# A graph network on one NeuronCore: TensorE's scatter loop in rounds of twenty groups, a different share of the marks for ScalarE, and three changed orders

## The reference, cut to what matters

```python
h = relu(layernorm(x)); x = x + gcn(h)         # L0: weighted sums over edges, degree normalised
h = relu(layernorm(x)); x = x + sage(h)        # L1: mean over edges, two 512x512 products, gate
h = relu(layernorm(x)); x = x + attention4(h)  # L2: four blocks of sparse attention and MLP
h = relu(layernorm(x)); x = x + gat(h)         # L3: two attention directions, fuse, batch norm
```

## Time and profile before

| What | us |
|---|---|
| Median of three runs (lowest and highest) | 882.91 (881.90 and 883.12) |
| The profiled execution's own time | 880.6 |
| Its span, from the first to the last instruction | 878.6 |
| PE busy, of the span | 826.9 (94%) |
| DVE busy | 623.1 (71%) |
| ACT busy | 460.1 (52%) |
| POOL busy | 493.6 (56%) |

### The profile page before, as it was taken

How to read it: one execution, slowest core, us unless ns; L and a number is a source line. 1 busy time by engine, 2 the same in 40 slices (tenths; PEclk the granted TensorE clock), 3 DMA queues, 4 the chain that set the end, 5 groups by cost and what they waited for, 6 DMA issues and landing times.

```text
span 878.6 us, 18172 instructions
## 1 busy us (share of the span) xinstructions
PE 826.9 (94%) x6778; PEld 723.7 (82%) x6778; DVE 623.1 (71%) x1271; ACT 460.1 (52%) x773; POOL 493.6 (56%) x542
## 2 busy tenths in 40 slices
PE   3999989999999999999999999999999999989896
PEld 2999868789898879998887989887898988875565
DVE  7998878964766683576766367577447667689996
ACT  5988675345762434565133466333447634256673
POOL 7354573678433577542466843266674338548871
PEclk9999999999999999999999999999999999999999
DMA  5000102233000142200024310003230002100121
GB/s 162 2 0 0 37 26 85 55 96 115 13 1 13 42 154 85 60 13 1 25 66 130 109 48 1 13 25 117 78 110 13 1 1 85 37 1 32 46 61 59
DMA packets 49760, 44.34 MB, mean 50 GB/s; under 512 B 6013, under 2 KB 37439, under 8 KB 49698
## 3 DMA queue, kind: packets, MB, share of 16 engines
q1 hardware_dynamic: 47234, 39.72, 15.2%
q10 hardware_dynamic: 2464, 3.80, 1.5%
HBM read 42.04 MB, written 1.33 MB: 49 GB/s over the span
## 4 chain that ended last, share of the span: by engine, by line
PE 70%; DVE 17%; ACT 6%; issue 3%; DMA 2%; DVEq 1%; POOL 0%; SPq 0%; ACTq 0%
PE psum L1822 20%; PE psum L1816 18%; PE psum L1927 13%; PE psum L1897 6%; PE psum L1846 5%; DVE arena L2349 3%; ACT arena L1618 2%; DVE arena L1013 2%; PE psum L2112 2%; PE psum L2109 2%; PE psum L1870 2%; PE psum L877 1%; PE psum L935 1%; DVE stats L2472 1%; DVE hot_dst L1050 1%
## 5 line engine op out<-in xcount | busy, mean ns | idle before, releaser
L1360 POOL TENSOR_SCALAR acc<-acc,rden,flag 128x628 f32<-128x628 f32 x80 | 69.5, 868 | 119.4 <-DVE rden L2345 119.4
L1927 PE MATMUL psum<-ringw,arena 128*128 128x512 f32 (+1 forms) x480 | 119.3, 397 | 4.0 <-DVE arena L2357 2.5
L1822 PE MATMUL psum<-arena 128*128 128x384 f32 (+5 forms) x675 | 115.8, 324 | 0.0
L1816 PE MATMUL psum<-arena,ringw 128*128 128x314 f32 x768 | 114.3, 310 | 0.1
L1816 PEld LDWEIGHTS psum<-arena,ringw 128*128 128x128 f32 x768 | 112.9, 190 | 1.5 <-DVE arena L2322 1.1
L1822 PEld LDWEIGHTS psum<-arena 128*128 128x128 f32 (+1 forms) x675 | 104.8, 189 | 7.1 <-DVE arena L2349 1.1
L1927 PEld LDWEIGHTS psum<-ringw,arena 128*128 128x128 f32 (+1 forms) x480 | 86.8, 186 | 25.6 <-DVE arena L2357 3.5
L1816 PE MATMUL psum<-arena 128*128 128x314 f32 (+1 forms) x480 | 87.7, 321 | 7.3 <-DVE arena L2349 6.9
L1816 PEld LDWEIGHTS psum<-arena 128*128 128x128 f32 (+1 forms) x480 | 70.5, 187 | 15.8 <-DVE arena L2349 14.1
L2322 DVE SCALAR_TENSOR_TENSOR arena<-psum,cols,arena 128x628 fp32r<-128x628 f32 x32 | 27.9, 872 | 75.8 <-ACT arena L1600 75.8
L1431 POOL TENSOR_TENSOR ringw<-raw,ringw 128x512 fp32r<-128x512 f32 x56 | 71.6, 1288 | 15.5 <-ACT ringw L1659 15.5
(11 more groups left out here) (313 smaller groups left out, 1840.6 us busy)
## 6 DMA issues: line engine op xcount, KB each, us to landing
raw<-in_L_gnn_m_w SPq DMA_DIRECT2D x16, 256.0 KB
xn<-in_L_gnn_m_w SPq DMA_DIRECT2D x16, 256.0 KB
raw<-in_L_gnn_wv SPq DMA_DIRECT2D x8, 256.0 KB
xn<-in_L_gnn_wv SPq DMA_DIRECT2D x8, 256.0 KB
raw<-in_L_gnn_wq SPq DMA_DIRECT2D x8, 256.0 KB
xn<-in_L_gnn_wq SPq DMA_DIRECT2D x8, 256.0 KB
raw<-in_L_gnn_wk SPq DMA_DIRECT2D x8, 256.0 KB
xn<-in_L_gnn_wk SPq DMA_DIRECT2D x8, 256.0 KB
```

The costliest lines, as they stand in the source:

```text
L1360: g.tensor_scalar(pbuf[:, k % 4, 0:NW], pbuf[:, k % 4, 0:NW], rden[:, k:k + 1], flag[:, 1, k % NT:k % NT + 1], ALU.mult, ALU.mult).then_in ...
L1816: ins = pe.matmul(big[buf(u)][0:l.shape[1], h, 0:HW], l, r[:, h * HW:(h + 1) * HW], start=(i == 0), stop=(i == len(terms) - 1))
L1822: ins = pe.matmul(to, l, r, start=(i == 0), stop=(i == len(terms) - 1))
L1927: ins = pe.matmul(brow(ROWBLK[f"{name}{t}"])[0:KEYS[t], :], l, r, start=(pieces[0] + i == 0), stop=(pieces[-1] == KT - 1 and i == len(term ...
```

## The change

There are five edits.

1. PE's scatter loop has bodies of ROUND = 20 groups instead of 4, so two rounds instead of ten.
2. ACT's and DVE's loops have bodies of SHARE = 8 groups. In the last group of each eight ACT makes chunks 2 and 3 and DVE only 0 and 1. ACT gets a third buffer for the extra Abs.
3. DVE's shift of `base_f` moves from the scatter's end to its start.
4. POOL makes `rstd_of` for tile 1 ahead of `left_rest(3)` instead of behind it, and `rstd_of` for tile 2 ahead of `bias_added(4)`.
5. In L3 PE waits for `h_read` and runs three idle products between `first_branch(0)` and `maxima(3)`.

```diff
--- before.py
+++ after.py
@@ -38,6 +38,13 @@
 assert all((i * PASS_MUL) >> 16 == i // WIN for i in range(NP + 1))
 HOT = 4
 assert NG % HOT == 0 and NT * 2 * WIN <= 512
+
+SHARE = 8
+assert NG % SHARE == 0 and SHARE % HOT == 0
+own_chunks = lambda g: CH - 1 - (g % SHARE == SHARE - 1)
+
+ROUND = 20
+assert NG % ROUND == 0 and ROUND % HOT == 0
 ACCW = NP + ROOM
 
 
@@ -274,7 +281,7 @@
         w_acc = adjacc[:, :, 1, 0:NP]
         hot_src = [m[:, :, :].rearrange("p t n -> p (t n)").bitcast(BF16)[:, b * CH * NP:(b + 1) * CH * NP].rearrange(
             "p (j n) -> p j n", j=CH) for m in (mask, z) for b in range(2)]
-        hot_abs = [mask[:, NT - 1, :].bitcast(BF16)[:, b * NP:(b + 1) * NP] for b in range(2)]
+        hot_abs = [mask[:, NT - 1, :].bitcast(BF16)[:, b * NP:(b + 1) * NP] for b in range(2)] + [xn[:, 1, D - NP // 2:D].bitcast(BF16)]
         hsum = hot_dst[:, :, :, :].rearrange("p b j n -> p (b j n)").bitcast(F32)[:, 0:NP].rearrange("p (t n) -> p t n", t=NT)
         cond_high = arena3[:, 0:NP]
         silu = xn[0:C16, :, :].rearrange("p b n -> p (b n)")[:, 0:NP]
@@ -912,6 +919,8 @@
             pe.wait_ge(am_read, 2)
             second_branch(1)
             first_branch(0)
+            pe.wait_ge(h_read, 2 * NT - 1)
+            idle_products(pe, 2 * NBIG, 3)
             maxima(EARLY)
             first_branch(1)
             pe.wait_ge(one_up, 2)
@@ -1515,11 +1524,12 @@
             for t in range(1, 4):
                 bias_added(t)
             left_rest(2)
-            rstd_of(LN_L1, NT)
+            for t in range(2):
+                rstd_of(LN_L1 + t, NT + t)
             left_rest(3)
-            rstd_of(LN_L1 + 1, NT + 1)
+            rstd_of(LN_L1 + 2, NT + 2)
             bias_added(4)
-            for t in range(2, NT):
+            for t in range(3, NT):
                 rstd_of(LN_L1 + t, NT + t)
             for k in range(KT):
                 right_rest(k)
@@ -1701,13 +1711,16 @@
             act.wait_ge(w_ready, 2)
             passes = act.value_load(span_i[0:1, 1:2], min_val=0, max_val=NP // WIN)
             with act.Fori(0, passes + 1) as kp:
-                with act.Fori(0, NG // HOT) as gi:
-                    for b in range(HOT):
-                        g = gi * HOT + b
+                with act.Fori(0, NG // SHARE) as gi:
+                    for q in range(SHARE):
+                        g, b = gi * SHARE + q, q % HOT
                         act.wait_ge(scat_full, kp * NG + g + 1)
-                        act.activation(hot_abs[b % 2][:, 0:NW], iota16[:, 0:NW], ACT.Abs, bias=src_col[:, CH - 1, bass.ds(g, 1)], scale=-1.0).then_inc(hot_abs_up, 1)
-                        act.wait_ge(hot_abs_up, kp * NG + g + 1)
-                        act.activation(hot_src[b][:, CH - 1, 0:NW], hot_abs[b % 2][:, 0:NW], ACT.Relu, bias=1.0, scale=-1.0).then_inc(hot_act_up, 1)
+                        for i, j in enumerate(range(own_chunks(q), CH)):
+                            to = hot_abs[q % 2 if i == 0 else 2]
+                            act.activation(to[:, 0:NW], iota16[:, 0:NW], ACT.Abs, bias=src_col[:, j, bass.ds(g, 1)], scale=-1.0).then_inc(hot_abs_up, 1)
+                            act.wait_ge(hot_abs_up, (kp * (NG // SHARE) + gi) * (SHARE + 1) + q + i + 1)
+                            ins = act.activation(hot_src[b][:, j, 0:NW], to[:, 0:NW], ACT.Relu, bias=1.0, scale=-1.0)
+                        ins.then_inc(hot_act_up, 1)
             wait_apart(act, scat_read, (passes + 1) * NG + HOT)
             def weights_high(t):
                 act.activation(adj[:, 0, t, :], w_acc[:, t, :], ACT.Copy).then_inc(whi_up, 1)
@@ -2092,9 +2105,10 @@
             pe.wait_ge(w_ready, 2)
             passes = pe.value_load(span_i[0:1, 1:2], min_val=0, max_val=NP // WIN)
             with pe.Fori(0, passes + 1) as kp:
-                with pe.Fori(0, NG // HOT) as gi:
-                    for b in range(HOT):
-                        c = kp * NG + gi * HOT + b + 1
+                with pe.Fori(0, NG // ROUND) as gi:
+                    for q in range(ROUND):
+                        b = q % HOT
+                        c = kp * NG + gi * ROUND + q + 1
                         to = scat(b)
                         pe.wait_ge(hot_src_up, c)
                         pe.wait_ge(hot_act_up, c)
@@ -2557,18 +2571,19 @@
             dve.wait_ge(hot_init, 3)
             passes = dve.value_load(span_i[0:1, 1:2], min_val=0, max_val=NP // WIN)
             with dve.Fori(0, passes + 1) as kp:
-                def hot(g, b):
+                def hot(g, q):
+                    b = q % HOT
 
                     dve.wait_ge(scat_full, kp * NG + g + 1)
                     def marks(j):
                         return dve.tensor_scalar(hot_src[b][:, j, 0:NW], iota16[:, 0:NW], src_col[:, j, bass.ds(g, 1)], None, ALU.is_equal)
 
-                    marks(0)
-                    marks(1)
+                    for j in range(own_chunks(q) - 1):
+                        marks(j)
 
                     dve.tensor_tensor(hot_dst[:, b, :, 0:WIN], iota16[:, 0:WIN].unsqueeze(1).broadcast_to([P, CH, WIN]),
                                       dst_rel[:, :, bass.ds(g, 1)].broadcast_to([P, CH, WIN]), ALU.is_equal).then_inc(hot_dst_up, 1)
-                    marks(2).then_inc(hot_src_up, 1)
+                    marks(own_chunks(q) - 1).then_inc(hot_src_up, 1)
 
                 def add(g, b):
 
@@ -2580,17 +2595,20 @@
 
 
                 dve.tensor_copy(base_i[:, :], base_f[0:1, :]).then_inc(pass_up, 1)
+                dve.tensor_scalar(base_f[0:1, :], base_f[0:1, :], float(WIN), float(NP), ALU.add, ALU.min).then_inc(pass_up, 1)
                 for b in range(HOT - 1):
                     hot(b, b)
                 wait_apart(dve, pass_up, kp * 3 + 1)
-                with dve.Fori(0, NG // HOT - 1) as gi:
-                    for b in range(HOT):
-                        hot(gi * HOT + b + HOT - 1, (b + HOT - 1) % HOT)
-                        add(gi * HOT + b, b)
-                hot(NG - 1, HOT - 1)
+                with dve.Fori(0, NG // SHARE - 1) as gi:
+                    for q in range(SHARE):
+                        hot(gi * SHARE + q + HOT - 1, (q + HOT - 1) % SHARE)
+                        add(gi * SHARE + q, q % HOT)
+                for g in range(NG - SHARE, NG - HOT):
+                    hot(g + HOT - 1, (g + HOT - 1) % SHARE)
+                    add(g, g % HOT)
+                hot(NG - 1, (NG - 1) % SHARE)
                 dve.wait_ge(hot_dst_up, kp * NG + NG)
                 dve.tensor_scalar(dst_rel[:, :, :], dst_rel[:, :, :], float(WIN), None, ALU.subtract).then_inc(pass_up, 1)
-                dve.tensor_scalar(base_f[0:1, :], base_f[0:1, :], float(WIN), float(NP), ALU.add, ALU.min).then_inc(pass_up, 1)
                 for b in range(HOT):
                     add(NG - HOT + b, b)
                 dve.wait_ge(pass_up, kp * 3 + 3)
```

## The result

| | us, median (lowest and highest) | Profiled execution, its span |
|---|---|---|
| Before, six runs beside the changed kernel's | 882.27 (881.64 and 883.12) | 880.6, 878.6 |
| After, six runs | 890.42 (888.27 and 891.45) | 890.63, 888.5 |

The changed kernel is slower: ratio 1.0087, 95% interval [1.0073, 1.0101], so 8.1 us more. The forecast was 3.4 less.

What follows compares the result with a forecast made beforehand. PE was taken as the bound, busy 826.9 of 878.6 us. Scatter -3.2, POOL's order -0.55 and L3 +0.3 gave -3.45, so 882.9 - 3.4 = 879.5 us (chance 45%); range 878.4 to 884.6.

Steps and rivals of the forecast that it cites:

- The step that failed: Scatter, PE's jump back at group 20: priced at 0.47 us, absorbed by slack that DVE leaves PE.
- Rival B: Scatter's jump back: two code fetches, 5.7 us, 884.4; 888 if the clock falls too; put at 885.5, chance 18%.
- From a back edge of 4.1 on the change loses: Scatter: the threshold, 4.1 us for PE's jump back, from which the change was to be slower than before.
- rivals A: Scatter's jump back must fetch its code once: 3.1 us for that back edge, 881.8 in all, chance 25%.
- two packets in the first round: Scatter before the change: two code packets fetched in the first round, none from 40 to 100 us.
- DVE's pace: Scatter: DVE with POOL need 1.743 us a group, 1.707 with the mark sharing; PE, at 1.70, runs into them.
- a longer round needs edit 2: Scatter: without ACT taking one mark in every eighth group from DVE, it would end 1.3 us later.
- ACT as the bound: Scatter: hand-over waits make ACT's pairs 1.77 us a group, 2.4 over forty groups: 881.9, chance 7%.
- Edit 3: Scatter's end: DVE's shift of `base_f` is off the path, 0 gained, 0.1 us paid at the start.
- Edit 4: Behind the scatter: DVE's first normalised tile falls from 1.12 to about 0.53 us; 0.55 gained, bounds 0 and 0.6.
- Edit 5: L3: idle products delay the maxima's copies about 0.7 us; 0.3 lost on DVE, bounds 0 and 0.4.
- can gain nothing: L3: the granted clock is full in this trace, so idle products gain nothing; in another execution they might.

Runs made afterwards that it cites:

- only20: The kernel before with only PE's scatter loop lengthened to rounds of twenty groups: 888.76 us, ratio 1.0088.
- round8: The changed kernel with PE's scatter rounds at eight groups instead of twenty: 880.33 us, ratio 0.9980 to the kernel before.
- head_first: The changed kernel, rounds of twenty, with the PE loop's first instruction at the start of a code packet: 886.95 us, ratio 1.0052 to the kernel before.
- hinted: The changed kernel, rounds of twenty, with a hint at PE's back edge that the branch will be taken: 885.94 us, ratio 1.0039 to the kernel before.
- round40: The changed kernel with all forty scatter groups of PE written out, no jump back: 881.80 us, ratio 1.0009 to the kernel before.
- round4: The changed kernel with PE's scatter rounds back at four groups, all else kept: 881.69 us, ratio 0.9997 to the kernel before.
- order_only: The kernel before with only POOL's new order of `rstd_of`: 881.83 us, ratio 0.9996.
- round8_no_idle: The changed kernel with PE rounds of eight groups and without L3's wait and idle products: 881.11 us, ratio 0.9983 to the kernel before.
- round8_scatter: The changed kernel with PE rounds of eight groups, without POOL's new order and L3's idle products: 881.00 us, ratio 0.9989 to the kernel before.
- idle_only: The kernel before with only L3's wait and three idle products on PE: 882.30 us, ratio 0.9998.

## Why the prediction was wrong

- **The step that failed** is "The back edge at group 20 falls into slack that DVE leaves PE and costs nothing more there", with its price of 0.47. That was the price of a jump over 480 instructions, taken for one over 2,400. Measured: 4.3 and 3.0, so 7.3. The branch of 4,151 ns in the changed kernel, 4,007 in only20 and 247 in round8 show it.
- **Rival B** named the outcome: two fetches in a row because of the late head, and the clock's fall behind them. head_first shows the first half of it, the windows the second. Its sizes were off both ways. A fetch was put at the 2.6 us of a small transfer, and the gap is 4.3 the first time and 3.0 the second, so 7.3 for 5.7. The clock's fall was put at 3.4, as if half the clock doubled the time, and cost about 1.5. The stops of the next point are not in it. So B was put at 885.5, 888 with the clock, where the median is 890.42; the range's upper end was 884.6. "From a back edge of 4.1 on the change loses" was too lenient: hinted, with one of 2.2, loses 3.6 us, since the stops at packet borders and the clock come on top. As a choice of chances the trace had too little against rivals A and B: nine short jumps show nothing of a far one.
- **A term that nobody had:** stops at packet borders in written-out code, 4.6 us in the changed kernel, 5.0 in round40 and 2.0 in only20, so half or all of the 4.2 of back edges that any longer body could save. With a body of four to twelve groups the code comes once and stays. I read two packets in the first round as free.
- **DVE's pace** held as far as it can be seen. round8 saves five of the nine back edges, 2.35, and PE then waits briefly at each group, as forecast for a PE that runs into DVE's and POOL's pace (that they are what it waits for at each of these is inferred from the one named wait); its scatter is 1.9 shorter. In the changed kernel nobody can see it, since behind the stop four groups lie ready. That a longer round needs edit 2, which the prediction put at 1.3 us, isn't tested: no run has a kept long body without it.
- **ACT as the bound** (rival C) is out: between 31 and 100 us one wait of 0.2 us is put down to it in round4, one in the kernel before and none in round8, and the one named at 70.96 was none.
- **Edit 3** is at 0 as far as the rows show, as forecast: the last add is still released by PE (no run has it alone). **Edit 4** gave its 0.6 (7.92 to 7.3), and in this pair of profiles gave it back at the mask step; the prediction followed POOL's later work to 123 us, and the meeting is at 145. **Edit 5** cost its 0.3 to 0.4, and the part "can gain nothing" rested on one execution with its clock full in L3. By their mean clocks most executions aren't like it, which the prediction left open.

## What to carry to other kernels

Here a written-out loop body of PE was kept up to seven code packets and not at nine, and a jump back over more has a price of its own: measure the branch at the length that you mean to use, not at the one you have. Count code packets (38 against 57 here): a loop whose body stays resident costs 0.47 us a turn, and code that is run once cost 0.1 to 0.3 us for each 250 instructions, with the engine issuing as densely as here. Take a length that is surely kept and that runs often: eight groups gave 1.7 us and twelve 1.1, which the intervals don't tell apart, and sixteen lost 7.

## What the runs showed of the hardware that was not expected

- A jump back to code that isn't there: a branch of 3.7 to 4.15 us, and 2.7 to 3.0 more where the head lies just ahead of a packet's end; with the head at a packet's start 3.8 us in one piece, and 2.2 with a hint at the back edge as well; nothing extra up to seven packets.
- At 1.2 GHz matmuls of 34 and 68 columns, each with its weight load, take a third more time than at 2.4, and not double: 0.11 us for three against 0.08.
- A stop of PE of 2.2 to 7.3 us in the midst of dense matmuls brought the clock to 1.2 GHz behind it in every profile that has one.
- A product of 64 x 512 on POOL that starts 0.03 us ahead of DVE's 128 x 640 mask step makes that 1.94 us for 0.82; when DVE is 0.07 ahead, POOL pays, 1.91 for 1.29.
- Without three products of PE whose result nobody reads, of under 0.3 us each, the clock in L3 was at 1.2 GHz for 3.4 to 6.8 us in the profiles of order_only, round8_no_idle and round8_scatter; with them it stayed at 2.4 in idle_only. The kernel before and only20, without them too, kept it in theirs.
